# Self-attention of a Perceiver block: values copied straight out of PSUM by ScalarE, their bias sent once through the output weights, the causal mask in float32r behind the value products

## What is computed

```python
x = x + xattn(layernorm(x), ctx, ctx, ...)      # 16 heads of 16, softmax over 256 keys
x = x + attn(layernorm(x), ...)                 # causal, 16 heads of 16, 64 keys
x = x + ffn(layernorm(x), ...)                  # quantised weights and activations, 1024 wide

def attn(x, w_qkv, b_qkv, w_out, b_out):
    q, k, v = split(x @ w_qkv + b_qkv)
    att = where(causal, heads(q) @ heads(k).T / 4, -inf)
    return (softmax(att) @ heads(v)) @ w_out + b_out
```

## Time and profile before

| | |
|---|---|
| median of 3 runs | 896.88 us (896.86 to 897.01) |
| the profiled execution | 896.43 us, its span 894.6 us |
| TensorE | 861.2 us busy, 96% of the span |
| VectorE | 745.5 us, 83% |
| ScalarE | 707.0 us, 79% |
| GpSimd | 483.2 us, 54% |
| mean granted TensorE clock | 0.996 |

### The profile page before, as it was taken

How to read it: one execution, slowest core, us unless ns; L and a number is a source line. 1 busy time by engine, 2 the same in 40 slices (tenths; PEclk the granted TensorE clock), 3 DMA queues, 4 the chain that set the end, 5 groups by cost and what they waited for, 6 DMA issues and landing times.

```text
span 894.6 us, 28711 instructions
## 1 busy us (share of the span) xinstructions
PE 861.2 (96%) x9750; PEld 724.1 (81%) x9750; DVE 745.5 (83%) x1551; ACT 707.0 (79%) x2077; POOL 483.2 (54%) x710
## 2 busy tenths in 40 slices
PE   7999999999999999999999988999999998999997
PEld 6888888888888889888888977888888885666664
DVE  6878878878878878878878776899999988999995
ACT  4788887777787777778777775888888877999996
POOL 3333334355454554433443226787878864777775
PEclk9999999999999999999999998999999999999999
DMA  6222111111111011111111100000000000000011
GB/s 193 91 90 84 42 47 30 43 49 35 36 47 41 30 47 41 47 29 41 47 41 30 36 1 2 2 3 0 0 1 0 1 1 2 29 32 30 30 36 35
DMA packets 31635, 31.84 MB, mean 36 GB/s; under 512 B 3280, under 2 KB 30800, under 8 KB 31568
## 3 DMA queue, kind: packets, MB, share of 16 engines
q1 hardware_dynamic: 30448, 30.47, 11.1%
q10 hardware_dynamic: 1120, 0.59, 0.2%
HBM read 26.86 MB, written 4.19 MB: 35 GB/s over the span
## 4 chain that ended last, share of the span: by engine, by line
PE 76%; ACT 11%; issue 5%; DVE 5%; POOL 2%; DMA 0%; DVEq 0%; ACTq 0%; POOLq 0%; SPq 0%
PE psum L349 12%; PE psum L319 9%; PE psum L304 9%; PE psum L336 8%; PE psum L375 6%; PE psum L681 5%; ACT probs L1056 3%; PE psum L719 3%; PE psum L730 3%; PE psum L387 3%; ACT probs L513 3%; PE psum L291 3%; PE psum L773 2%; PE psum L700 2%; PE psum L357 2%
## 5 line engine op out<-in xcount | busy, mean ns | idle before, releaser
L513 ACT ACTIVATE probs<-psum,nmax 128x256 f32<-128x256 f32 x512 | 237.3, 487 | 89.9 <-DVE nmax L470 89.9
L470 DVE TENSOR_REDUCE nmax<-psum 128x2 f32<-128x512 f32 x256 | 158.8, 683 | 7.5 <-PE psum L336 7.3
L544 POOL TENSOR_TENSOR rm<-rinv,hm_sb 128x256 f32<-128x256 f32 x64 | 39.7, 621 | 214.8 <-DVE rinv L447 214.8
L349 PE MATMUL psum<-id_sb,probs 128*128 128x128 f32 x1024 | 126.6, 275 | 0.5
L537 POOL TENSOR_TENSOR cl<-c_sb,ch 128x512 fp32r<-128x512 f32 x64 | 81.6, 1275 | 77.6 <-ACT ch L488 77.6
L349 PEld LDWEIGHTS psum<-id_sb,probs 128*128 128x128 f32 x1024 | 114.4, 141 | 4.0 <-ACT probs L513 4.0
L494 ACT ACTIVATE probsT<-psum 128x512 f32<-128x512 f32 x160 | 89.4, 614 | 33.8 <-PE psum L349 32.5
L513 ACT ACTIVATION_READ_ACCUMULATOR probs<-psum,nmax 128x1 f32 x512 | 112.3, 219 | 0.0
L336 PE MATMUL psum<-k_sb,qb 32*128 32x256 f32 x1024 | 81.3, 401 | 4.2 <-DVE qb L431 1.2
L440 DVE COPY probsT<-psum 128x512 f32<-128x512 f32 x96 | 65.5, 682 | 11.2 <-PE psum L349 9.3
L336 PEld LDWEIGHTS psum<-k_sb,qb 32*128 32x128 f32 x1024 | 53.9, 184 | 21.5 <-issue 15.6
(11 more groups left out here) (155 smaller groups left out, 2389.4 us busy)
## 6 DMA issues: line engine op xcount, KB each, us to landing
c_sb<-in_ctx_t SPq DMA_DIRECT2D x64, 256.0 KB, 2.8
x_sb<-in_x SPq DMA_DIRECT2D x32, 128.0 KB, 2.5
out<-y_sb SPq DMA_DIRECT2D x32, 128.0 KB, 1.7
w_all<-in_w_gate SPq DMA_DIRECT2D x1, 1024.0 KB, 5.1
w_all<-in_w_up SPq DMA_DIRECT2D x1, 1024.0 KB, 6.7
w_all<-in_w_down SPq DMA_DIRECT2D x1, 1024.0 KB, 5.9
wqkv_sb<-in_w_qkv SPq DMA_DIRECT2D x1, 768.0 KB, 5.2
wk_sb<-in_wk ACTq DMA_DIRECT2D x1, 256.0 KB, 4.0
```

Of the source, the lines that this page charges most:

```text
L349: last = nc.tensor.transpose(sp[g][:, c:c + P], probs[:, 2 * g + u, kh * P:(kh + 1) * P], id_sb[:])
L470: nc.vector.tensor_reduce(nmax[:, 2 * g:2 * g + 2], sp[g].rearrange("p (u s) -> p u s", u=2), AX.X, ALU.max, negate=True).then_inc(max_don ...
L513: nc.scalar.activation(probs[:, j, :], sp[g][:, u * S:(u + 1) * S], ACT.Exp, bias=nmax[:, j:j + 1], accum_out=rsum[:, j:j + 1]).then_inc(e ...
```

## The change

Four edits, which go together:

1. The value bias is no longer added to the values. Since softmax rows sum to one, it passes the attention unchanged, so it is put through the output weights once and added to the output bias: in cross-attention's tile 9 TensorE multiplies a broadcast of it with `wout_sb` (`pe_bias`, two fp32 matmuls of 256 columns), and VectorE adds the product to `bout_sb` (`dve_bias`). Before tile 9 VectorE writes the broadcast into `oT2` (`dve_bias_rows`). TensorE's value product of that tile and GpSimd's first use of `bout_sb` wait for `bias_done`.
2. `dve_v2` and `v2b` are gone. ScalarE copies the values from PSUM (`v2_ps`) into one of two `v2` buffers, one tile earlier in its order; TensorE's waits for `v2b_done` become waits for `v2_ev`, and the last `act_v2` leaves the crossing to the feed-forward part.
3. The mask's two matmuls are a function of their own, `pe_mask2`, and stand for tile t+2 between its values and the value product of tile t.
4. The mask's operands live in `x1l` and `x1h`, float32r buffers that cross-attention no longer needs, so the product is float32r and not bfloat16, and the mask's large number is 1e38.

```diff
-        id2_b = sb("id2_b", [P, 2, L], BF16)
-        ca_b = sb("ca_b", [P, 8, L], BF16)
+        v2 = [sb(f"v2{s}", [P, 2, D]) for s in range(2)]
+        id2_b = x1l[:, 0, 0:P].rearrange("p (a b) -> p a b", b=L)
+        ca_b = x1h[:].rearrange("p k (a b) -> p (k a) b", b=L)
...
         def pe_v2(pe, t, s, j):
             pe.wait_ge(xl_done, t + 1)
-            pe.wait_ge(v2b_done, t)
+            pe.wait_ge(v2_ev, t * 4)
...
-        def pe_scores2(pe, t, n, s, j):
-            pe.wait_ge(qq_ev, n * 2 + 2)
-            pe.wait_ge(kbd4_pool, t + 1)
+        def pe_mask2(pe, t):
             pe.wait_ge(sub_done, t)
             for r in range(2):
                 nc.tensor.matmul(sc_ps[r], id2_b[half(r)].rearrange("p a b -> p (a b)"),
                                  ca_b[half(r)].rearrange("p a b -> p (a b)"),
                                  start=True, stop=False)
+        def pe_scores2(pe, t, n, s, j):
+            pe.wait_ge(qq_ev, n * 2 + 2)
+            pe.wait_ge(kbd4_pool, t + 1)
+            pe.sem_inc(s2_ready, 1)
...
-            nc.vector.tensor_tensor(v2b[par][:], v2_ps, bv2_sb[:], ALU.add).then_inc(v2b_done, 1)
+        def pe_bias(pe, t):
+            pe.wait_ge(bias_set, 1)
+            pe.wait_ge(o_ev, t * 2 + 1)
+            for k in range(KT):
+                last = nc.tensor.matmul(bias_ps, oT2[:, k, :], wout_sb[:, k, :],
+                                        start=k == 0, stop=k == KT - 1)
+            last.then_inc(bias_mm, 1)
+        def dve_bias(v):
+            v.wait_ge(bias_mm, 1)
+            nc.vector.tensor_tensor(bout_sb[:], bias_ps, bout_sb[:], ALU.add).then_inc(bias_done, 1)
...
         def act_v2(a, t, par):
-            a.wait_ge(v2b_done, t + 1)
-            a.wait_ge(pv2_mm, t)
+            a.wait_ge(v2_mm, t + 1)
+            if t > 1:
+                a.wait_ge(pv2_mm, t - 1)
...
                     if ahead5:
-                        pe.wait_ge(v2b_done, t + 2)
+                        pe.wait_ge(v2_ev, (t + 2) * 4)
                         pe_xt2(pe, t + 5, x0_ps)
...
                         pe_v2(pe, t + 2, there, i % 2)
-                    pe_pv2(pe, t)
+                        pe_mask2(pe, t + 2)
+                    pe_pv2(pe, t, i % 2)
...
                 def body2(t):
-                    act_v2(a, t, t % 2)
+                    if t > 0:
+                        act_v2(a, t + 1, (t + 1) % 2)
...
                 act_xqt(a, 1)
-                act_v2(a, NT - 1, 1)
                 act_r2(a, NT - 1)
```

More of the change, by code:

```diff
@@ L634, in block_kernel @@
         v2_ev = sem("v2_ev")
-        v2b_done = sem("v2b_done")
+        bias_set = sem("bias_set")
+        bias_mm = sem("bias_mm")
+        bias_done = sem("bias_done")
         kbd4_pool = sem("kbd4_pool")
+        s2_ready = sem("s2_ready")
         s2_mm = sem("s2_mm")
@@ L811, in dve_y2, with dve_bias_rows @@
             nc.vector.tensor_tensor(at(t), y2_ps, at(t), ALU.add).then_inc(y2_ev, 1)
[L813 to L816, removed]
-            nc.vector.tensor_tensor(v2b[par][:], v2_ps, bv2_sb[:], ALU.add).then_inc(v2b_done, 1)
+        bias_ps = op[:, D:2 * D]
+        def dve_bias_rows(v):
+            v.wait_ge(w2_in, 16 * len(SET2))
+            nc.vector.tensor_copy(oT2[:], bv2_sb[:].unsqueeze(2).to_broadcast([P, KT, P]))\
+              .then_inc(bias_set, 1)
+        def pe_bias(pe, t):
[8 more added lines that the diff above has]
+            nc.vector.tensor_tensor(bout_sb[:], bias_ps, bout_sb[:], ALU.add).then_inc(bias_done, 1)
         def act_xt2(a, t, s, j, turned):
@@ L1190, in _, with body @@
                 pe_scores(pe, 0, 0, 0, 0)
-                def body(t, n, j, first=False, wsum=False, ahead2=True):
+                def body(t, n, j, first=False, wsum=False, bias=False, ahead2=True):
                     pe_k(pe, t, 1)
@@ L1210, in body @@
                         pe_wsum(pe, t)
+                    if bias:
+                        pe_bias(pe, t)
                     pe_v(pe, t + 1, 0, (1,))
@@ L1214, in body @@
                         pe.wait_ge(wscale, 1)
+                    if bias:
+                        pe.wait_ge(bias_done, 1)
                     pe_pv(pe, t, 1)
@@ L1224, in _ @@
                 body(8, 4, 0, wsum=True)
-                body(9, 4, 1)
+                body(9, 4, 1, bias=True)
                 with pe.Fori(5, NT // 2 - 1) as n:
@@ L1269, in body2 @@
                     if ahead1:
+                        if first:
+                            pe_mask2(pe, t + 1)
                         if i % 2:
@@ L1348, in _ @@
                 nc.vector.memset(ones[:], 1.0).then_inc(const_set, 1)
-                nc.vector.memset(v2[:], 0.0).then_inc(const_set, 1)
+                for w in v2:
+                    nc.vector.memset(w[:], 0.0).then_inc(const_set, 1)
                 nc.vector.memset(eps_col[:], EPS).then_inc(const_set, 1)
@@ L1368, in _, with body @@
                 dve_max(v, 0, 0)
-                def body(t, n, j, first=False, scale=False, ahead2=True, ahead3=True):
+                def body(t, n, j, first=False, scale=False, bias=False, ahead2=True, ahead3=True):
                     if not first:
@@ L1391, in body @@
                         dve_wscale(v)
+                    if bias:
+                        dve_bias(v)
                     dve_k(v, t + 1, 0)
@@ L1403, in _ @@
                 body(8, 4, 0, scale=True)
-                body(9, 4, 1)
+                dve_bias_rows(v)
+                body(9, 4, 1, bias=True)
                 with v.Fori(5, NT // 2 - 2) as n:
@@ L1564, in _ @@
                 act_k2(a, 0, 0)
+                a.wait_ge(const_set, 4)
+                act_v2(a, 0, 0)
                 act_pt(a, t, 1)
@@ L1570, in _ @@
                 act_r(a, t, 1)
+                act_v2(a, 1, 1)
                 act_xt2(a, 3, 1, 1, x0_ps)
@@ L1698, in _ @@
                 pool_xl(p, 3, 1, 1)
+                p.wait_ge(bias_done, 1)
                 for i in range(4):
```

36 lines of the change are left out of this document (15 added, 21 removed).

## The result

| | before | the change |
|---|---|---|
| median | 896.94 us (895.23 to 898.57, 6 runs) | 901.41 us (901.18 to 903.54, 6 runs) |
| ratio | | 1.0052, 95% interval 1.0038 to 1.0067 |
| profiled execution | 896.43 us, span 894.6 | 901.42 us, span 899.6 |

What follows compares the result with a forecast made beforehand. TensorE's own list of matmuls was taken to bound the kernel. Terms +2.7 + 1.3 + 0.1 - 1.05 = +3.05 on the profiled 896.43 gave 899.5, with the median 0.45 higher 899.9 us; range 896.5 to 902.8.

Steps and rivals of the forecast that it cites:

- The mask: Self-attention on TensorE: a float32r mask weight load shows behind the shape change, 0.10 us in each of 27 tiles, +2.7 us.
- what would show it: Signs: mask load near 188 ns, matmul near 480, 6.3 us a tile, values to mask 0.2, mask to value product 0.4.
- load hidden: Rival in self-attention: TensorE loads the float32r mask weights under the values; sum 0.35, 897.2 us, chance 0.12.
- values and mask as one: Rival in self-attention: load and shape change both hidden, saving 0.10 us in each of 27 tiles; 894.5 us, chance 0.12.
- halves in turn: Rival in self-attention: the mask's two halves run one after the other, 5.9 us more, 905.8 us, chance 0.05.
- The bias product: Cross-attention: the product, VectorE's sum and the key bias delay the scores by 1.3 us, once; ends +0.9 and +1.7.
- the later row maxima pass something on: Cross-attention: the reason given for the bias term's upper end, +1.7 us.
- The values: VectorE's sum goes at three places near the feed-forward part, -0.84, and ScalarE's last copies, 0.2; together -1.05 us, ends 0 and -1.8.
- the rivals of ScalarE and VectorE as bounds: ScalarE's value copies hold TensorE, 909 us, chance 0.05; VectorE was the bound after all, 7 us faster, chance 0.01.
- The wait that I had named: Where the feed-forward part's norm is mixed in: TensorE waits 0.82 us for the low part of the output.
- The crossing: Between cross-attention and self-attention: the transposes wait for ScalarE's second value copy and the longer mask, +0.1 us.
- a longer stretch of low clock: One reason for the range's upper end, 902.8; a shift in the crossing can change the half-clock stretch by about 1 us.

Runs made afterwards that it cites:

- the shifted kernel before: The kernel before with one unused tile of 32 bytes a partition ahead of wout_sb, moving all tiles behind it; 897.92 us, ratio 1.0013.
- the best version: The changed kernel with the mask in bfloat16, bias product and sum in the crossing, and two unused 32-byte tiles; 895.14 us, ratio to before 0.9966.

## Why the prediction was right, and where not

**The mask.** Right in kind and nearly in size: a float32r load that shows behind each change of shape. Forecast 0.10 us a tile, measured 0.11 (0.43 against 0.32). I gave it to 27 tiles; it counts in 29 of the 31 steps, so 3.3 us (2.85 to 3.32 by three pairs of traces) for 2.7. Of what would show it, the steps hold (0.21 from values to mask, 0.43 behind it, 6.3 a tile, no idle time of TensorE before the transposes of x); the load is 183 ns for my 188, and the matmul 498 for my 480. The three rivals on the mask (load hidden; values and mask as one; halves in turn) are out by the 0.43, the 0.21 and again the 0.43. (Under the first I had said that loads of 188 ns hide under steps of half that; the steps are 117 ns.) By the Trainium skill ("TensorE: Matmul & The Clock Gate", Weight-path perf modes) the fast load is for types other than FP32; with 183 ns against 92 for the same 128 columns in bfloat16, float32r falls with FP32 here.

**The bias product.** Forecast +1.3, and r 8b to r 10b takes 1.85 us more. The 1.85 are 0.68 for the product, 0.56 for the key bias behind the sum (shown by moving it), and 0.61 at the transposes of x. The first two are the waits that I had summed. The 0.61 looks like the delay of VectorE, paid for a second time, but 0.41 of it comes with three instructions ahead of the loop and no bias at all. That leaves some 0.20 for the delay, an estimate by difference. It fits the end that I had named and left out of the value taken, "the later row maxima pass something on": VectorE's row maxima start 1.05 us ahead of r 9b before (179.97 and 181.02) and 0.83 in the change (181.83 and 182.66). So the bias itself cost about 1.44, within its ends of 0.9 and 1.7.

**The values.** The copies on ScalarE are hidden, as forecast: it waits 27.0 us for TensorE and no one for it, so the rivals of ScalarE and VectorE as bounds are out. VectorE's sum and what hangs on it gave 1.47 us and not 1.05, between two kernels of one layout, the shifted kernel before and the one with the bfloat16 mask (195.24 to 193.89 from first to last mask, and 0.12 behind it). By the scores, which kept their place, it lies where I had looked for it: 0.57 in the step from scores 29 to 30 (7.03 to 6.46) and 0.69 behind the last scores, with 0.09 in the second tile of self-attention. The wait that I had named is shorter too, beside the 0.82 of the earlier trace rows:

```profile
752.09 0.48 PE L779 MATMUL psum<-w2oh,oh 128*128 128x256 f32 x2 [0.46 <-POOL ol L920]
```

Tile 31 comes sooner by about what I had said: from the value product of tile 26 to that of tile 31 it is 31.25 us before and 30.07 in the change (-1.18). The masks hide this, as they moved: mask 26 to the last is 30.54 for 30.80.

**The crossing.** Forecast +0.1, measured -0.05 to the first mask and +0.06 to the first scores in this pair, which happened to have the same clock (0.69 and 0.57 for 0.68 and 0.57 in the two dips).

**What the sum lacked.** The forecast terms as measured are 3.32 + 1.44 - 0.05 - 1.35 - 0.13 (the last row of the table) = +3.23. The spans differ by 5.0. The rest, some 1.76, is in no term: layout +0.35 + 1.09 - 0.81 = +0.63, and the place of VectorE's loop, +0.41 in its first turn and +0.72 in the later ones. The parts of self-attention add up by the way in which they were taken; those of cross-attention are from separate kernels. I had read the smaller `bv2_sb` as a saving in a transfer, and didn't look at what is declared behind it. That the range held is in part luck: it was wide toward a longer stretch of low clock, a reason that did not occur, and these effects filled it.

## What to carry to other kernels

A float32r operand in place of a bfloat16 one costs its weight load wherever the tile shape changes ahead of it; count those places before sharing a buffer for it. Place work that happens once where the engines idle: the bias product cost about 1.4 us in tile 9, and in the crossing nothing that shows (30.45 us for 30.44). When an edit moves an instruction, don't measure with that one; take one whose place is the same in both kernels. And before costing the edit, look at what it moves without naming: the addresses of all tiles behind a resized one, and the place of each loop in its engine's program. Here these made some 1.76 of 5.0 us. A wait that appears beside new work need not come from it: half a microsecond of tile 9 looked like the bias and was mostly the loop's place.

## What was new about the hardware

- The address of tiles by 32 bytes: with `ch` and `cl` 32 bytes off a multiple of 64, float32r weight loads take 191 ns for 188 and projection steps 119.8 for 117.1 ns, seen in eight traces. With the tiles on a multiple it is 117.1 to 117.4, and 118.2 in the best version (medians of 117 in all). The key projection (line 304) slows down too, to steps of 120 ns for 117 and loads of 192 for 188 (medians), though its weights `wkh` and `wkl` did not move and only its moving operand did. So the operand that is loaded need not be the one that is off. Self-attention is then 0.6 to 0.8 us faster instead, for which no tile was found.
- The place of a loop in an engine's program: three instructions ahead of VectorE's loop put 0.38 us between two instructions in the first turn and 0.08 in each later one. Kernels with one instruction more kept steps of 8.26 to 8.28 us, those with three took 8.35 to 8.37, and 8.67 in the first turn without bias work. In the feed-forward part the kernel with three instructions more, and the one without the bias, were 0.85 us faster than those they are compared with. That fetching of instructions is behind it was not tested.
- The clock in the crossing: with the same order and an idle time of 2.0 us ahead, the granted clock was 1.00 in one execution and 0.62 in another (mean of 4 us), and the crossing 28.85 and 30.34 us. Over the fourteen traces the crossing takes 28.74 to 31.63 us. The 75 runs of before beside the experiments spread from 894.8 to 899.7 us: those with a mean granted clock of 0.997 or more took 894.8 to 895.9, those with 0.994 or less 898.0 to 899.7. How much of that lies in the crossing, single traces can't say.
